# The first phase of a two-layer graph network in natural block order: x in seven transfers, degrees by sets, table rows split and stored inside the projection

## What is computed

```python
x = x + _L0_gnn_ref(_layernorm(x, axis=-1), edge_index, ...)

def gcn_conv(x, edge_index, W, b):          # src, dst: edges and self-loops
    deg = jax.ops.segment_sum(jnp.ones_like(dst, dtype=x.dtype), dst, num_segments=n)
    dinv = jnp.where(deg > 0, jax.lax.rsqrt(deg), 0.0)
    norm = dinv[src] * dinv[dst]
    h = x @ W.T
    msgs = norm[:, None] * h[src]
    out = jax.ops.segment_sum(msgs, dst, num_segments=n)
    return out + b
```

## Time and profile before

| | us |
|---|---|
| median of 3 runs | 6411.74 |
| lowest, highest | 6405.93, 6443.31 |
| span of the profiled execution | 5133.3 |
| first phase in it (first instruction to the start of the second phase) | 192 |

### The profile page before, as it was taken

The page is one execution under the profiler, slowest core; times in us unless marked ns, Lnnn a source line. Parts: engine busy times, 40 slices in busy tenths (PEclk is TensorE's granted clock), DMA queues, the critical chain, the costliest instruction groups (busy, mean ns, idle before and its releaser), DMA issues. The chain is left out here.

```text
span 5133.3 us, 76751 instructions
## 1 busy us (share of the span) xinstructions
PE 3775.5 (74%) x19865; PEld 2844.9 (55%) x19865; DVE 3388.9 (66%) x9213; ACT 2416.2 (47%) x7596; POOL 3451.8 (67%) x3620
## 2 busy tenths in 40 slices
PE   6277777777777777775676777777777777768998
PEld 4156666666566666654454555555555555545665
DVE  6655555555555555554788888888788888874454
ACT  5323333333333333333576666666666666661222
POOL 4377777777777777774777777777777777732222
PEclk9589999999999999898777677777677677768999
DMA  4655655656555566663555555555555555534221
GB/s 132 202 161 170 171 170 170 170 170 170 169 170 167 169 171 170 170 170 97 139 150 154 150 150 152 149 150 148 152 146 155 149 149 153 150 92 149 75 78 48
DMA packets 338812, 767.24 MB, mean 149 GB/s; under 512 B 79990, under 2 KB 178392, under 8 KB 338238
## 3 DMA queue, kind: packets, MB, share of 16 engines
q0 software_dynamic: 202704, 594.02, 41.8%
q1 hardware_dynamic: 135662, 168.07, 10.0%
HBM read 712.95 MB, written 58.60 MB: 150 GB/s over the span
## 5 line engine op out<-in xcount | busy, mean ns | idle before, releaser
L826 POOL DMA_INDIRECT flow_rows<-table,edges x1708 | 1625.4, 952 | 609.0 <-issue 499.0
L1430 POOL DMA_INDIRECT gat_steps_rows<-table,edges x1712 | 1627.7, 951 | 558.5 <-issue 488.1
L1864 PE MATMUL gat_steps_sum_ps<-gat_steps_rows,gat_steps_onehot 128*128 128x264 f32 x3424 | 1149.9, 492 | 270.4 <-DVE acc L1584 258.1
L1173 PE MATMUL flow_sum_ps<-flow_rows,flow_onehot 128*128 128x256 bf16 x5124 | 767.1, 290 | 430.3 <-DMA flow_rows<-table,edges 343.9
L1864 PEld LDWEIGHTS gat_steps_sum_ps<-gat_steps_rows,gat_steps_onehot 128*128 128x128 f32 x3424 | 780.9, 240 | 488.1 <-DVE acc L1584 302.1
L1173 PEld LDWEIGHTS flow_sum_ps<-flow_rows,flow_onehot 128*128 128x128 bf16 x5124 | 497.7, 104 | 628.4 <-issue 299.9
L1731 ACT ACTIVATE gat_steps_rows<-gat_steps_rows 128x64 f32<-128x64 f32 x3424 | 828.6, 334 | 0.0
L899 DVE TENSOR_TENSOR acc<-flow_sum_ps,acc 128x256 f32 x854 | 360.2, 422 | 659.8 <-PE flow_sum_ps L1173 638.7
L1584 DVE TENSOR_TENSOR acc<-gat_steps_sum_ps,acc 128x264 f32 x856 | 370.1, 432 | 275.6 <-PE gat_steps_sum_ps L1864 200.6
L1225 PE MATMUL flow_y_ps<-flow_w,flow_hid 128*128 128x256 f32 x1568 | 434.9, 402 | 85.8 <-DVE flow_x_blk L985 44.7
L1215 PE MATMUL flow_hid_ps<-flow_xn_t,flow_w 128*128 128x128 f32 x3136 | 457.2, 293 | 11.1 <-ACT flow_hid L1108 10.9
(11 more groups left out here) (382 smaller groups left out, 5390.7 us busy)
## 6 DMA issues: line engine op xcount, KB each, us to landing
gat_steps_drow<-drow SPq DMA_DIRECT2D x107, 512.0 KB
gat_steps_rows<-table,edges POOLq DMA_INDIRECT x1712
flow_rows<-table,edges POOLq DMA_INDIRECT x1708, 3.1
expert_w<-in_L_ffn_w SPq DMA_DIRECT2D x16, 1024.0 KB, 7.4
table<-start_parts SPq DMA_DIRECT2D x49, 192.0 KB, 1.8
gat_steps_mask<-masks SPq DMA_DIRECT2D x428, 12.1 KB
table<-flow_row SPq DMA_DIRECT2D x49, 130.0 KB, 2.5
gat_steps_self_row<-table SPq DMA_DIRECT2D x49, 130.0 KB
```

The costliest lines, as they stand in the source:

```text
L826: nc.gpsimd.indirect_dma_start(out=rows[n % RING][:, t, :], out_offset=None, in_=g["table0"][:, :], in_offset=bass.IndirectOffsetOnAxis(ap ...
L1173: ins = t.matmul(sum_ps[i % 2][:, :], onehot[i // AHEAD % 2][:, i % AHEAD * T + u, :], rows[i % RING][:, u, part * D:(part + 1) * D], star ...
L1430: nc.gpsimd.indirect_dma_start(out=rows[w % RING][:, t, 0:RW], out_offset=None, in_=g["table1"][:, :], in_offset=bass.IndirectOffsetOnAxis ...
L1864: ins = t.matmul(sum_ps[(w * SPW + s) % BANKS][:, :], onehot[k][:, i, :], rows[r][:, i, :], start=(i == s * T), stop=(i == s * T + T - 1))
```

## The change

- The blocks of the first phase are processed in natural order. x comes in 7 transfers of 7 blocks (`load`), the first ahead of W, without an address from a register.
- The ranks (`ranks`, `places`, `orders`, `step_ranks` on VectorE) come between the first sets' statistics; `reach_i` for the degree gathers is made first.
- GpSimd gathers the degree rows of sets 0 and 1, then the 14 edge gathers, then sets 2 to 6. Then `own_rows`: 49 multiplications that write `dinv * row` into `acc` at the block's rank, with the rank from a register.
- Degrees are worked out set by set: two matmul pairs (`steps`), `degrees`, a square root (`degree_root`) and `inverse`.
- `keep` writes the projected row over x in `g["x"]`. ScalarE's loop has 71 iterations now (`LAG` = 21): 21 iterations after a block's normalisation ScalarE makes its high part (`high`), and one iteration later its middle part (`middle`); VectorE makes `rest` and `low`. VectorE has one loop of 10, with `split(m - 3)` in iteration m.
- `edge_work` and `keep_edges` start two sets later (`FIRST` = 2). The masks come in iteration 7 of VectorE's loop, the flags in iteration 8.
- SyncE stores the table rows of a set in their natural place between the other stores.
- `masks`, `ends`, `span` and the flags' tiles lie where the degree rows lay; `parts` has a place of its own.

```diff
-        EDGES_AT = (1, 3, 5)
+        EDGES_AT = (2, 4, 6)
+        LAG = 3 * SET
+        FIRST = 2
...
-        left = xn
+        left = [sb(f"left{k}", [P, D]) for k in range(3)]
...
 # GpSimd
+            def own_rows(m):
+                _, at = nc.values_load_multi_w_load_instructions(
+                    rank_of_block[0:1, m * SET:(m + 1) * SET], engines=[pool.engine], min_val=0, max_val=(NB - 1) * RA,
...
+                pool.wait_ge(dinv_known, m + 1)
+                for i in range(m * SET, (m + 1) * SET):
+                    pool.wait_ge(rows_kept, i + 1)
+                    nc.gpsimd.tensor_tensor(g["acc"][:, bass.ds(at[i - m * SET], D)], g["x"][:, i, :],
+                                            dinv_n[:, i:i + 1].broadcast_to([P, D]), ALU.mult).then_inc(self_ready, 1)
...
+            pool.wait_ge(reach_known, 1)
+            degree_rows(0)
+            degree_rows(1)
             pool.wait_ge(groups_known, 1)
...
+            for m in range(2, SETS):
+                degree_rows(m)
+            pool.wait_ge(blocks_known, 1)
+            for m in range(SETS):
+                own_rows(m)
 # SyncE
+            def load(m):
+                c = slice(m * SET, (m + 1) * SET)
+                sp.dma_start(g["x"][:, c, :], a["x"].rearrange("(b p) d -> p b d", p=P)[:, c, :]).then_inc(x_in[m], 16)
...
+            load(0)
             sp.dma_start(w_in[:, :, :], a["L0_gnn_W"].rearrange("(o p) k -> p o k", p=P)).then_inc(w_loaded, 16)
-            sp.wait_ge(blocks_known, 1)
-            for m in range(SETS):
-                for i, at in enumerate(rows_of(nc, sp, g, m * SET, SET, 0)):
-                    sp.dma_start(g["x"][:, m * SET + i, :], a["x"][bass.ds(at, P), :]).then_inc(x_in[m], 16)
+            for m in range(1, SETS):
+                load(m)
+            sp.wait_ge(consts, 1)
...
 # VectorE
+            def rest(i):
+                k = i % 3
                 dve.wait_ge(high_ready, i + 1)
...
+                at_least(dve, parts_ready, i - 2)
+                v.scalar_tensor_tensor(left[k][:, :], g["x"][:, i, :], dinv_n[:, i:i + 1], parts[i % DEEP][:, 0, :], ALU.mult,
+                                       ALU.subtract).then_inc(left_ready, 1)
+
+            def low(i):
+                dve.wait_ge(left_ready, i + 1)
+                dve.wait_ge(mid_ready, i + 1)
+                v.tensor_tensor(parts[i % DEEP][:, 2, :], left[i % 3][:, :], parts[i % DEEP][:, 1, :], ALU.subtract
+                                ).then_inc(parts_ready, 1)
...
             set_stats(0)
+            ranks()
+            set_scales(0)
             set_stats(1)
-            set_scales(0)
+            places()
             set_scales(1)
...
+            for m in range(SETS + 3):
+                if 0 < m < SETS - 1:
+                    set_scales(m + 1)
+                if 0 <= m - 2 < SETS:
+                    inverse(m - 2)
+                if m + 2 < SETS:
+                    set_stats(m + 2)
+                if m == FIRST:
+                    dve.wait_ge(edges_in, 32 * SQ)
+                if 0 <= m - FIRST < SQ:
+                    edge_work(m - FIRST)
+                if m == SETS:
                     tile_masks()
...
+                if 0 <= m - 3 < SETS:
+                    split(m - 3)
+                if m == SETS + 1:
+                    flags()
+                if 0 <= m - 1 < SETS:
+                    degrees(m - 1)
+                if m == 0:
+                    orders()
+                if m < SETS:
+                    count_set(m)
+                if m == 0:
+                    step_ranks()
 # ScalarE
+            def high(i):
+                if i % SET == 0:
+                    act.wait_ge(dinv_known, i // SET + 1)
+                act.wait_ge(rows_kept, i + 1)
                 at_least(act, rows_out[i % DEEP], 16 * (i // DEEP))
...
+                s.activation(parts[i % DEEP][:, 0, :], g["x"][:, i, :], ACT.Copy, scale=dinv_n[:, i:i + 1]).then_inc(high_ready, 1)
+
+            def middle(i):
+                act.wait_ge(left_ready, i + 1)
+                s.copy(parts[i % DEEP][:, 1, :], left[i % 3][:, :]).then_inc(mid_ready, 1)
...
-            for i in range(NB + 2):
+            for i in range(NB + LAG + 1):
...
+                if 0 <= i - LAG < NB:
+                    high(i - LAG)
+                if 0 <= i - LAG - 1 < NB:
+                    middle(i - LAG - 1)
+                if at in EDGES_AT and 0 <= m - FIRST < SQ:
+                    keep_edges(3 * (m - FIRST) + EDGES_AT.index(at))
 # TensorE
+            def steps(m):
+                pe.wait_ge(set_counted, m + 1)
+                for n in range(2):
+                    t.matmul(reach_ps[m][:, n, :], step_back[:, :], reach[:, n, 1 + m * SET:1 + (m + 1) * SET], start=True, stop=False)
+                    ins = t.matmul(reach_ps[m][:, n, :], corner[:, :], reach[:, n, m * SET:(m + 1) * SET], start=False, stop=True)
+                ins.then_inc(steps_ready, 1)
...
+                if at == SET - 1 and 0 <= m - 1 < SETS:
+                    steps(m - 1)
```

277 lines of the change are left out of this document (142 added, 135 removed).

## The result

The changed kernel takes 6431.2 us in the median of 20 runs (6414.6 to 6448.8), the kernel before 6416.4 in 20 runs (6398.4 to 6443.3). The ratio is 1.0023, 95% interval 1.0013 to 1.0032: 15 us slower, and by the bound of one per cent it is no change. The prediction was 6412 with a range of 6370 to 6442, "same" at 0.93. The class is right and the range holds the time. The sum behind it is not right: it says 0 us, and the phase that was changed became 21 us longer. The forecast's own narrower range of 6395 to 6430 is missed by 1 us; 6431.2 lies nearer to the two slower rivals (6438 and 6439).

The account below looks back on a forecast made before the run. GpSimd's gathers fill most of the span; the change can move only the first phase ahead of them, at most 192 us. Phase -6, clock +5, GpSimd's disturbance +1 gave 0, so 6412 us, range 6370 to 6442.

Parts of the forecast that it names:

- the two slower rivals: First phase: TensorE staying at 1.2 GHz (6438, chance 0.15), or GpSimd's multiplications holding vector instructions (6439, chance 0.07).
- Head: Start of the first phase: early x lets the first block reach TensorE at 26.2 instead of 39.5, 13 us earlier.
- Loops 0 to 2: VectorE's first loops: statistics, counts and a wait for edges and TensorE, so that loop 3 begins at 65.
- An iteration with an edge transpose stays 2.6: ScalarE's projection iterations: the 0.97 us it already stands still for TensorE covers the new instructions' 0.7.
- Free, unless they slow VectorE: GpSimd's 49 multiplications after the gathers: off the path, disturbance 0 to 15 us, 1 us taken.
- the port rival: Shared SBUF interfaces: each of 49 multiplications holds a vector instruction up to 0.56 us, 27 at most; 6439, chance 0.07.
- SP's queue holds nothing late ... each behind at most 7 stores: Loops 7 to 9: masks go out at 154, ends back by 163, flags after them, none late.
- Waits for stores ... add 4: Loops 7 to 9: a store may not keep 0.8 us a block, so waits add 4 us.
- Surcharge for the clock: Projection sets: TensorE idles 5 to 6 us in each and its clock falls; 0 to 32 us, 5 taken.
- The rival at the lower clock: Projection: TensorE stays at 1.2 GHz, iterations 0.65 us longer, 26 us slower in all; 6438, chance 0.15.
- The 1278 us: Whole kernel: median of the runs above the profiled span of 5133 us, unexplained by the trace, taken as unchanged.
- the signs named for being right: First phase: first block at 25 to 28, ScalarE and VectorE waits, statistics near 21 us apart, first gather at 182 to 202.

Follow-up runs that it names:

- e3: Changed kernel with 28 extra unused 128x128 matmuls on TensorE in front of blocks 23, 30, 37 and 44; 6452.13 us in one execution.
- e1: Changed kernel without GpSimd's 49 multiplications, acc filled with zeros instead; 6419.89 us in one execution.
- e2: Changed kernel with masks and drow stored from GpSimd's queue instead of SyncE's; 6431.26 us in one execution.
- e5: Changed kernel with tile masks written and stored in pieces during the projection's loops, through two small buffers; 5152.65 us, ratio to before 1.0042.
- e6: Changed kernel with the 49 own-row multiplications moved from GpSimd to VectorE; 5162.33 us, ratio to before 1.0065.
- e7: Changed kernel with both edits, masks in pieces and own rows on VectorE; 5157.09 us, ratio to before 1.0058.
- e8: e7's kernel with VectorE's work for its set spread in sevenths ahead of each split; 6382.14 us, ratio to before 0.9970.
- e9: e8's kernel with table rows split two sets and two blocks behind the projection instead of three sets; 6393.91 us, ratio to before 0.9983.

## Why the prediction was right, and where its sum was not

| step of the prediction | predicted | trace, lower level |
|---|---|---|
| first projected block | 26.2 | 26.02 |
| loop 3 starts | 65 | 69.2 |
| loops 3 and 4, each | 21.4 | 24.2 |
| loops 5 and 6, each | 18 | 20.3 |
| loop 7 | 20 (144 to 164) | 29.5 (158.1 to 187.6) |
| from there to the phase's end, tail included | 21.8 | 25.9 |
| phase's end | 185.8, 191.8 with surcharges | 213.54 |

*Head: right.* 13.5 us were gained on the lower level, as worked out.

*Loops 0 to 2: 4 us short.* VectorE waited 10.72 us for TensorE at 64.25. The place and the wait were right, its size was 3 us too small. TensorE was granted 0.51 of its clock in 55 to 60 and 1.00 in 60 to 64, so part of that is the lower level.

*Loops 3 and 4: the mechanism right, a term mis-sized.* "ScalarE can't run ahead while VectorE does statistics, edge work and counts" is what the rows show, and a plain iteration of 1.7 us is 1.72. The term that failed is "An iteration with an edge transpose stays 2.6": it took 3.79. The 0.97 us of waiting did not cover the new instructions; ScalarE has them in front of the edge copy and the wait behind them grew to 1.69. Three such iterations a set are 3.6 us more, which more than holds the 2.8 that were missing; the clock's share (e3: 0.8 us a set) is among them.

*Loops 5 and 6: GpSimd.* "Free, unless they slow VectorE": they do. The count took 4.15 instead of 1.92, the splits' instructions 0.83 instead of 0.42. The 1 us that I took for it was some 8 to 9 in all (e1), 4.1 of them in these two loops: inside my 0 to 15, and the port rival's mechanism at a third of its 27 us. That instructions of the split go over 0.5 us while GpSimd multiplies stood among my signs of being wrong, and it came. The Trainium skill had said it: the page GPSIMD Engine Reference (Key points) states that GpSimd shares its SBUF interfaces with VectorE and contends with vector instructions that run in a 2-port perf mode or have two SBUF inputs. The traces agree for the split's two-input instructions (0.83 instead of 0.42 us). Comparisons of one tensor with a scalar per partition were slowed too; whether they ran in such a mode no trace here shows. With 28 multiplications in a row VectorE stood for 11.16 and 16.29 us in one instruction. A multiplication took 0.57 us in a run with VectorE held (16.03 us for 28), and 0.72 in the mean of the changed kernel. That agrees with the estimate of 0.56 from the Trainium skill (GPSIMD Engine Reference, Elementwise, side-by-side cycle accounting).

*Loop 7: the step that failed most.* "SP's queue holds nothing late ... each behind at most 7 stores" looked at the queue and asked whether the masks, ends and flags would be late. The question was what they do to the table rows behind them. ScalarE waited 9.54 us for a buffer, and the last set's degrees, which stand behind these splits on VectorE, with it. "Waits for stores ... add 4" was 17.3 us in the trace (9.54, 1.16, 6.56). e2 shows that another queue for the masks doesn't help. The traces put most of the 9.54 us behind the ends' 8-byte packets, 6 us at about a sixth of the rate, and some 4 us on the masks' own bytes; the 6.56 us are the flags on one DMA engine. e5, with the masks in pieces during the projection, loses the first wait and not the second.

*Surcharge for the clock: about right.* 5 us taken, about 3 by e3, whose filler matmuls cost something themselves. The rival at the lower clock (6438) came near the measured time, but not for its reason: with the granted clock at 0.94 the sets stayed at 23.5 us.

*The 1278 us.* Taking them as unchanged was harmless here, as the loss on the upper level (14.8 us) is near that of the lower (20.6 in the phase). Whether the difference between them is real I can't say: no trace of the kernel before exists on the upper level.

So the range held because everything at stake was 0.8% of the time, and because it was drawn out to the rivals; that is luck as far as the sum goes. Two of the signs named for being right failed, too: the interval between statistics near 21 us (24.2) and the first gather at 182 to 202 (214.16). In the phase itself the sum was off by 21.7 us (191.8 to 213.54): 4.2 in loops 0 to 2, 9.9 in loops 3 to 6, 9.5 in loop 7 and 4.1 behind it, less the 6 of surcharges that these already hold.

## What to carry to other kernels

When a stage is laid into a loop whose engines wait for each other in order, don't add up each engine's work: find the longest stretch in which one engine serves nobody, and cut that into pieces between its deliveries; this turned sets of 27 us into sets of 19. For each transfer that a change puts late, look at its packets as well as its bytes, and at what stands behind it on the same DMA engines, whichever queue issues it: here 14 KB in 8-byte packets were followed by 6 us of slow transfers, and 107 KB that went over one engine held the rows back longer than drow's 448 KB. And don't give GpSimd a backlog of elementwise work beside a busy VectorE.

## What the runs showed of the hardware that I had not expected

- A run of 28 GpSimd multiplications (128x256, 0.57 us each) held one VectorE instruction until its end, or nearly: 16.29 us where both began together, 11.16 us, and 11.67 us for seven comparisons that ended 1.7 us after it. In the changed kernel, with 35 in 23.5 us, VectorE's instructions got through at 0.83 us each. What decides between the two wasn't tried.
- It goes the other way too: a gather that takes GpSimd 0.95 us took 2.53 once, at 31.43 in the changed kernel, while VectorE counted.
- For about 6 us behind 1792 stores of 8 bytes (`ends`), packets of 1.5 KB took 0.42 to 0.48 us in the mean instead of 0.07, in eleven traces; the 16 engines were full at 59 to 71 GB/s. Whether the 8-byte stores cause it wasn't tried.
- A store of 107 packets of 1 KB (`flags`) ran one packet behind another for 5.5 us, where drow's 896 packets of 512 bytes took 1.7. ScalarE got its row buffer 0.91 to 0.93 us after the last of them in ten traces.
- Reading seven positions into registers cost VectorE 1.4 us of idle time per set (9.9 us in seven places in e6).
- The same program ran at 5.13 and at 6.42 ms. The gathers' durations are equal (954 and 951 ns); what differs is the idle time between them (541.5 against 962.5 us in the second phase of the changed kernel), and the first set's degrees come 29 us later while gathers run without a break (28 to 63 us). The expectations speak of a chip of one level or the other, but e5 to e7 (lower) and e8 and e9 (upper) were recorded under the same chip number. The cause stays open.
